# The top-k's transposes, value products and output turns, two beats later in the hand-written beat order

## The reference

```
scores = jnp.einsum('bqhd,bkhd->bhqk', q, k) / jnp.sqrt(jnp.float32(D))
top_s, top_i = jax.lax.top_k(scores, TOPK)          # TOPK = 16, 77 keys
attn = jax.nn.softmax(top_s, axis=-1)
o = jnp.einsum('bhqk,bhqkd->bqhd', attn, vg)         # vg: the values at top_i
```

## Time and profile before

| | |
|---|---|
| median of three runs | 2875.61 us |
| the profiled execution's own time | 2865.66 us |
| its span | 2864.3 us |
| mean granted TensorE clock | 0.916 |
| PE busy over the span | 2413.2 us (84%) |
| DVE busy over the span | 1737.0 us (61%) |
| first scores of the top-k to the end of `topk_rest` | about 271 to 712 us |

### The profile page before, as it was taken

One profiled execution on the slowest core, in us unless ns is written; L12 is line 12 of the kernel. 1 busy time (PEld: TensorE's weight loads), 2 busy tenths in 40 slices (PEclk: granted clock), 3 DMA queues, 4 the chain that ended last, 5 costly groups with the idle time before them and its releaser, 6 DMA issues.

```text
span 2864.3 us, 37279 instructions
## 1 busy us (share of the span) xinstructions
PE 2413.2 (84%) x13127; PEld 1239.1 (43%) x13127; DVE 1737.0 (61%) x5398; ACT 1278.7 (45%) x2434; POOL 338.8 (12%) x350
## 2 busy tenths in 40 slices
PE   6768677978888879999888899988889988889768
PEld 2455334444555444554344445442234332234335
DVE  5645856566334565657857666657676677775344
ACT  2324434434222213555535545545646646656434
POOL 3101332233120110000200000000000010000201
PEclk8889788889899888999989999998999989999979
DMA  4656231000000130000422100042120032110120
GB/s 162 172 119 189 86 115 39 17 15 14 4 8 24 50 83 12 12 23 12 133 61 73 42 16 12 12 132 88 48 44 12 23 107 83 42 27 12 41 62 15
DMA packets 150927, 160.66 MB, mean 56 GB/s; under 512 B 33391, under 2 KB 120258, under 8 KB 150476
## 3 DMA queue, kind: packets, MB, share of 16 engines
q1 hardware_dynamic: 150740, 158.28, 19.3%
HBM read 97.39 MB, written 60.19 MB: 55 GB/s over the span
## 4 chain that ended last, share of the span: by engine, by line
PE 65%; DVE 17%; ACT 6%; DMA 4%; issue 3%; POOL 2%; SPq 2%; ACTq 0%; POOLq 0%; DVEq 0%
PE bank L1145 9%; PE bank L1646 8%; PE bank L1117 7%; PE bank L1092 7%; PE bank L1667 5%; PE bank L2120 4%; PE bank L1121 3%; PE bank L756 3%; PE bank L1568 3%; PE bank L2297 3%; DVE max L1218 2%; DVE bank L1215 2%; PE bank L2122 2%; ACT work L1159 2%; PE bank L683 2%
## 5 line engine op out<-in xcount | busy, mean ns | idle before, releaser
L1159 ACT ACTIVATE work<-bank 128x512 f32<-128x512 f32 (+1 forms) x1216 | 701.5, 596 | 585.3 <-PE bank L1121 261.1
L1215 DVE CUSTOM_DVE_ANT_0 bank<-bank,weights 128x512 f32<-128x512 f32 x512 | 349.2, 702 | 198.7 <-PE bank L1092 197.1
L1218 DVE TENSOR_REDUCE max<-bank 128x1 f32<-128x512 f32 x512 | 340.6, 685 | 138.2 <-PE bank L1092 136.0
L1092 PE MATMUL bank<-k_stack,q_stack 97*128 97x512 bf16 x896 | 362.1, 406 | 68.4 <-DVE max L1215 28.2
L1117 PE MATMUL bank<-q_stack,k_stack 99*128 99x512 bf16 x896 | 345.3, 388 | 13.2 <-ACT work L1159 9.5
L1646 PE MATMUL bank<-hT,weights 128*128 128x512 f32 x512 | 266.0, 620 | 13.0 <-ACT work L1692 6.6
L1121 PEld LDWEIGHTS bank<-ident_b,weights 128*128 128x128 bf16 x2048 | 159.6, 98 | 119.2 <-issue 10.3
L1092 PEld LDWEIGHTS bank<-k_stack,q_stack 97*128 97x128 bf16 x896 | 89.7, 100 | 270.5 <-DVE max L1215 101.6
L1121 PE MATMUL bank<-ident_b,weights 128*128 128x128 bf16 x2048 | 200.2, 220 | 0.0
L1667 PE MATMUL bank<-weights,work 128*128 128x256 f32 x768 | 196.7, 384 | 0.0
L756 PE MATMUL bank<-hT,weights 128*128 128x512 f32 x288 | 156.9, 642 | 12.3 <-ACT hT L717 9.3
(11 more groups left out here) (242 smaller groups left out, 3656.2 us busy)
## 6 DMA issues: line engine op xcount, KB each, us to landing
q_stack<-parts_q SPq DMA_DIRECT2D x60, 384.0 KB, 3.9
parts_q<-parts SPq DMA_DIRECT2D x46, 384.0 KB, 2.6
k_stack<-parts_k SPq DMA_DIRECT2D x40, 384.0 KB, 4.9
weights<-parts_q SPq DMA_DIRECT2D x36, 384.0 KB, 4.0
parts_q<-parts SPq DMA_DIRECT2D x46, 256.0 KB, 2.9
parts_k<-parts SPq DMA_DIRECT2D x24, 384.0 KB, 2.5
parts_k<-parts SPq DMA_DIRECT2D x24, 256.0 KB, 2.9
weights<-in_L_e_w SPq DMA_DIRECT2D x12, 512.0 KB, 5.6
```

The costliest lines, as they stand in the source:

```text
L1092: m = pe.e.matmul(bank.ap[:, :], self.q(g)[0:MAX_ROW, h, qt * P:(qt + 1) * P], k_stacks[self.key, g].ap[0:MAX_ROW, h, half * BLK:(half + 1 ...
L1159: ac.e.activation(p.ap[0:self.nk, :], banks[self.key, "exp", g, i].ap[0:self.nk, :], ACT.Exp).then_inc(*probs.tick((self.key, g, i)))
L1215: ve.e.tensor_tensor_reduce(bank[:, :], bank[:, :], mask_bias[:, qt, half * BLK:(half + 1) * BLK], 1.0, -3.4e38, ALU.add, ALU.max, to).the ...
L1218: ve.e.tensor_reduce(to, bank[:, :], AX_X, ALU.max).then_inc(*maxima.tick((self.key, g, i)))
```

## The change

Nothing is added and nothing removed: five lags of `TopK` grow by two beats, on PE, ACT and DVE, and the length of both top-k stages grows by two beats (80 to 82, 208 to 210). The scores, DVE's four steps, the exponentials, POOL's two operations and SP's loads keep their beats.

```diff
--- before.py
+++ after.py
@@ -1237,7 +1237,7 @@
             def __init__(self, units, stacks_free):
                 self.units, self.stacks_free = units, stacks_free
                 self.groups = sum(u.groups for u in units)
-                self.beats = self.lead + self.period * self.groups + 11
+                self.beats = self.lead + self.period * self.groups + 13
 
             def at(self, g):
                 return self.units[g // 4], g % 4
@@ -1263,13 +1263,13 @@
                     if now := self.group(beat, 0, 16):
                         if now[1] % 4 == 0:
                             self.scores(pe, *self.at(now[0]), now[1] // 4)
-                    if now := self.group(beat, 7, 16):
+                    if now := self.group(beat, 9, 16):
                         if now[1] % 4 == 0:
                             self.turn(pe, *self.at(now[0]), now[1] // 4, turns)
                             turns += 1
-                    if now := self.group(beat, 20, 1):
+                    if now := self.group(beat, 22, 1):
                         self.pv(pe, *self.at(now[0]))
-                    if now := self.group(beat, 22, 1):
+                    if now := self.group(beat, 24, 1):
                         u, g = self.at(now[0])
                         bank = banks.take(self.bank("exp", turns), (u.key, "turn", g), (vec, (u.key, "out", g)))
                         u.finish_turn(pe, g, bank)
@@ -1344,7 +1344,7 @@
                             ac.wait_ge(*turned[k])
                             ac.e.activation(work[k, "prob"].ap[0:LC, :], banks[k, "turn"].ap[0:LC, :], ACT.Copy).then_inc(
                                 *probs.tick((k, "turned")))
-                    if now := self.group(beat, 21, 1):
+                    if now := self.group(beat, 23, 1):
                         u, g = self.at(now[0])
                         u.finish_copy(ac, g)
                     yield
@@ -1356,7 +1356,7 @@
                     if now := self.group(beat, 1, 16):
                         u, g = self.at(now[0])
                         self.keep_16(ve, (u.key, g, now[1] // 4), now[1] // 4, now[1] % 4)
-                    if now := self.group(beat, 23, 1):
+                    if now := self.group(beat, 25, 1):
                         u, g = self.at(now[0])
                         u.finish_out(ve, g)
                     yield
```

## The result

The kernel after takes 2854.49 us (median of 20 runs, 2846.26 to 2867.57) where the kernel before, run beside it, takes 2871.82 us (20 runs, 2862.61 to 2881.51). The ratio is 0.9944, 95% interval 0.9933 to 0.9954: 16 us faster. The forecast was 2871.3 us with a range of 2857 to 2884. (Against the 2875.61 us of the three first runs, 3.8 us of the miss are the base.)

The account below looks back on a forecast made before the run. Neither PE nor DVE was full in the top-k stretches; the binding engine alternates. Terms -1.0 - 3.5 - 1.1 - 1.4 + 1.8 + 0.9 gave -4.3 us: 2861.4 from the profiled 2865.66, plus 9.95 to the median, 2871.3; range 2857 to 2884.

Parts of the forecast that it names:

- All 39.8 us of turn waits: PE's waits at the turns (L1303) in both top-k stages, 39.8 us, the most to win; sign: under 15 us.
- rival B: DVE rules wherever PE waited, so waits only move and the time stays 2875.6 us within 3; chance 0.20.
- Part 1, the place at L2076: Turn wait at 461.09 us: scores come ahead, so DVE's 11.41 us idle ends sooner; credit 3.5 us, range 0 to 5.
- Part 2, the copy that pv needs: Fourth turn's copy stands three beats behind the exponentials, so pv waits less; half of 2.7 us credited, 1.4.
- The other turn waits: Remaining turn waits in both stages, where DVE is full or the stage's end keeps its order; credit 0.
- Part 4, the longer stage: Part after DVE's last top-k step grows two beats, so dense work loses DVE's cover; charge 0.9 us, second stage nothing.
- Part 3, L957 behind an exponential: Copy L957 falls behind an exponential and PE waits for it at L964; charge 1.8 us, range 0 to 25.
- Rival C: Fewer stalls also raise PE's clock in a 20 us stretch of each stage: 12 us more, 2859 us; chance 0.16.
- C's sign: A mean granted clock over 0.85 in the first stretch (first top-k stage) would show that the clock pays too.
- Rival D: Slower: PE waits at L964 at most group ends, with the dense lane behind it: +10 us, 2885; chance 0.24.
- After 712 us: Behind the top-k stretch: a change of more than 5 us there would be none of the prediction's steps.

Follow-up runs that it names:

- e6: Kernel before with only pv, the copy L957, the finishing transposes (L964) and finish_out two beats later, turns unmoved, stages 80 and 208 beats: ratio 0.9964.
- e9: Kernel before with the change's lags only for group 4 of the second top-k stage (tiles 32 to 35): ratio 0.9988.
- e1: Kernel before with the change (lags and 82 beats) in the first top-k stage only: ratio 0.999 to the kernel before.
- e5: Kernel before with the change's lags only for groups 5 to 8 of the second top-k stage (tiles 36 to 51): ratio 1.001.
- e4: The change's lags in both stages, stages kept at the old 80 and 208 beats: ratio 0.9932 to the kernel before.
- e14: The change with the first top-k stage kept at 80 beats, the second at 210: ratio 0.9931 to the kernel before.
- e7: The change's lags at 80 and 208 beats, with the copy L957 ahead of the next exponentials again: ratio 0.9922 to the kernel before.
- e12: The change's lags, copy L957 ahead of the next exponentials, stages of 79 and 207 beats: ratio 0.991 to the kernel before.
- e10: All lags one beat later than in the kernel before, stages of 80 and 208 beats: ratio 0.9978.
- e11: Against the kernel before, turns three beats later, pv and what follows four, stages of 81 and 209 beats: ratio 0.9939.
- e16: The change's lags, copy L957 ahead of the next exponentials, stages of 80 and 207 beats: ratio 0.9917 to the kernel before.

## Why the prediction was wrong, step by step

- **"All 39.8 us of turn waits", credited where DVE idles behind.** The waits fell as foretold, to 13.5 us (under 15 was the sign), and much of it only moved, as rival B has it: L683's waits on DVE grew by 9.6 us, L964's on ACT by 6.0, and L1568's on POOL's gated tile from 5.9 to 7.3.
- **Part 1, the place at L2076** (credit 3.5). Right. From the last L1709 ahead of it (447.13 before, 450.81 after) to the end of DVE's long idle were 30.24 us, now 24.98: 5.3 us less. The rows of PE and then of DVE, to be held against the earlier trace rows:

```profile
471.51 4.03 PE L2076 MATMUL bank<-weights,work 128*77 128x512 f32 x9
475.37 0.31 PE L1291 MATMUL bank<-kx_stack,q_stack 96*128 96x77 bf16 x4
```
```profile
475.79 0.68 DVE L1391 MAX8 top<-bank 128x8 f32<-128x77 f32 x4 [10.10 <-PE bank L1291]
```

  The scores stand right behind the run of L2076, as worked out. Counted from tile 16 instead, the end of that idle comes 3.7 us earlier (93.9 us behind it before, 90.2 now). All of tiles 16 to 36 kept 2.3 us of it.
- **Part 2, the copy that pv needs (credit 1.4). This is the step that failed**: the term was mis-sized, because the sum put the clock at nothing. I priced pv's three waits at half their own length. They stand at the head of the experts and in them (524.98, 551.90 and 577.41 us), where PE has 4.5 us of idle time in 75.7 and so everything counts, and the first stood where the granted clock had just come up. The experts gained 9.1 us: 6.6 by PE's busy time, 2.5 by its idle time. e6 (pv moved, turns not) has 8.8 us of it and e9 (one group) 5.7 us. Of the 6.6 us the relapse behind the first wait is 4.3 (e1 to e9, e5 to e4).
- **The other turn waits, credit 0 where DVE is full.** Wrong in the first stage: e4 and e14 take 7.1 us off it. The prediction read too much into the earlier trace rows: DVE was full from 281.77 to 313.68 us (the row at 317.51 has 3.83 us of idle ahead of it), which is 31.9 us and not 35, and only 6.6 of the stage's 21.3 us of turn waits stood in them. PE had 37.1 us of idle in the stage and a clock of 0.77; of the 7.1, some 2.4 are PE's busy time and 4.6 its idle time, while the turn waits fell by 5.3. The longest of them, 5.12 us at 336.33, stayed (5.57 us in e4), with DVE busy in 4.78 of its 5.12 us. Which move in the order gives the gain is open. The change itself hid this miss by the next one.
- **Part 4, the longer stage (charge 0.9).** Also mis-sized: 6.3 us in the first stage by e14. "The part behind DVE's last step" was taken as dense work that loses its cover. The runs show it as a longer end of the stage, tiles 12 to 16 in 49.9 us with the change and 42.7 with e14; what of it is order and what clock is open. For the second stage, nothing, it was right.
- **Part 3, L957 behind an exponential (charge 1.8).** Right in kind: L964's waits grew by 6.0 us. Its price is not shown to be other than nothing: e7 takes such waits away (6.1 to 0.9 us) and tiles 0 to 63 stay at 404.4 us. That was tried at 80 and 208 beats, not in the change itself.
- **The clock.** Rival C had the mechanism. The half-speed stretch it named, 300 to 320 us, stayed slow: the clock went from 0.50 to 0.66 where the same work lies now, 303 to 323 us, and the first stretch stayed at 0.77 (0.78 before), against the 0.85 set as C's sign. The clock came back where I had not looked, at 526 us. The Trainium skill's page "TensorE: Matmul & The Clock Gate" (What's actually happening) says that activity releases the throttle; e9, where one wait less left the clock at 1.00, agrees. But L2120 also waited 1.21 us for L2314, up to 523.77, in the kernel after (1.35 in e12), and the clock held; which wait costs the clock and which doesn't, no run here shows.
- **Rival D**'s waits are real at another lag: e10, 18.6 us at L964. The two beats of this change miss it by one.
- **After 712 us** nothing over 5 us, as said: the profiled pair stands 9.3 us apart at the top-k's last write-out (710.05 and 700.73 us) and 8.0 at the end.

## What to carry to other kernels

Where an in-order engine has a heavy operation every few beats, a lag is to be judged by its remainder in that rhythm, not by its length: one beat gave 0.9978, two 0.9932, three 1.0009 and three with pv at four 0.9939, and each time something else stood right behind the exponentials (with one beat the copy L957, with three the turn's copy). A stall in a stretch where PE is nearly full should be priced with the granted clock of the microseconds behind it (one 1.37 us wait went with 4.3 us of PE's busy time behind it), and a look at short windows of that clock belongs ahead of any sum. If lags need more room, lengthen the stage only when the last one does not fit: here the old 80 beats held the new lags.

## What the runs showed of the hardware that was not expected

The same code in the same order can cost PE 10 us more or less. From 2680 us on, where the last big loads begin, the order is the same in all of these kernels. Before:

```profile
2680.00:2810.00 130.00, 82.75 (x446) 46.73 (x446) 64.05 (x190) 43.52 (x77) 23.32 (x29) 0.79 0.20 57
```

e5, which had won 6.3 us in the experts and showed nothing in its time:

```profile
2681.70:2820.00 138.30, 93.05 (x448) 51.86 (x447) 64.49 (x191) 44.50 (x77) 23.32 (x29) 0.72 0.19 53
```

PE is busy 10.3 us longer with the same matmuls, at a granted clock of 0.72 instead of 0.79, and the stretch takes 8.3 us more. The change took 132.5 us for it, at 0.77.

All eighteen traces show it. Counted from the same write-out (L980) at 2683.23 us in the kernel before to the last one, 92.6 us later there, the stretch takes 92.6 to 101.5 us with the same 347 or 348 matmul records:

| kernel | us | PE busy | granted clock |
|---|---|---|---|
| before | 92.6 | 58.5 | 0.76 |
| e11 | 92.7 | 57.8 | 0.78 |
| the change | 93.4 | 59.5 | 0.74 |
| e4 | 99.1 | 66.8 | 0.65 |
| e16 | 101.5 | 69.1 | 0.64 |

e16, with the shortest top-k stretch of all, gives 8.9 us back here against the kernel before. So a single profiled execution can hide or fake a gain of the size of this change; why the clock differs there isn't shown. Whether it belongs to a kernel or to an execution isn't shown either, as each kernel was profiled in one. That the runs of one kernel spread over 0.7 to 1% may have this cause, which was not tested.
